# A recurrent two-tower network of 128 steps on one core: the opening's tiles, loads and orders rewritten

## The reference

```python
def _leaky(x):                      # NEG = 0.2
    return jnp.where(x >= 0, x, NEG * x)

def _tower(x, w_in, b_in, blocks):  # two blocks, all widths 128
    h = _leaky(x @ w_in + b_in)
    for w1, b1, w2, b2 in blocks:
        h = _leaky(_leaky(h @ w1 + b1) @ w2 + b2 + h)
    return h

def step(prev_delta, xk):
    fk, k = xk
    d = jnp.where(k == 0, fk[:, DELTA_IDX], jax.lax.stop_gradient(prev_delta))
    fk = fk.at[:, DELTA_IDX].set(d)
    fe = _tower(fk[:, :N_FLAT], fw_in, fb_in, flat_blocks)   # 4 features, needs d
    pe = _tower(fk[:, N_FLAT:], pw_in, pb_in, path_blocks)   # 8 features, does not
    h = _leaky(jnp.concatenate([fe, pe], axis=-1) @ cw1 + cb1)
    delta = jax.nn.sigmoid(h @ cw2 + cb2)[:, 0]
    return (delta, delta)
```

## Time and profile before

| what | us |
|---|---|
| median of 3 runs | 1250.41 |
| the three runs | 1250.08, 1250.41, 1253.89 |
| the profiled execution | 1254.54 |
| its span, first to last instruction | 1252.7 |
| PE, DVE, ACT busy in it | 1247.0, 890.9, 931.0 |

### The profile page before, as it was taken

How to read it: one execution, slowest core, us unless ns; L and a number is a source line. 1 busy time by engine, 2 the same in 40 slices (tenths; PEclk the granted TensorE clock), 3 DMA queues, 4 the chain that set the end, 5 groups by cost and what they waited for, 6 DMA issues and landing times.

```text
span 1252.7 us, 19624 instructions
## 1 busy us (share of the span) xinstructions
PE 1247.0 (100%) x6028; PEld 1063.5 (85%) x6028; DVE 890.9 (71%) x1950; ACT 931.0 (74%) x2049; POOL 11.8 (1%) x28
## 2 busy tenths in 40 slices
PE   9999999999999999999999999999999999999998
PEld 6888888888888888888888888888888888888886
DVE  3777777767777777777777777777777777777775
ACT  3777777777777777777777777777777777777776
POOL 1000000000000000000000000000000000000000
PEclk9999999999999999999999999999999999999999
DMA  2000000000000000001000000000000000000000
GB/s 75 30 10 31 13 10 30 13 30 10 24 20 11 29 13 24 17 10 33 11 23 19 12 30 10 30 13 11 29 14 29 10 21 22 11 23 12 13 4 1
DMA packets 14881, 24.50 MB, mean 20 GB/s; under 512 B 1983, under 2 KB 8214, under 8 KB 14782
## 3 DMA queue, kind: packets, MB, share of 16 engines
q1 hardware_dynamic: 13982, 22.33, 5.5%
q10 hardware_dynamic: 720, 0.66, 0.2%
q0 software_dynamic: 80, 0.26, 0.1%
HBM read 16.67 MB, written 6.55 MB: 19 GB/s over the span
## 4 chain that ended last, share of the span: by engine, by line
PE 98%; DMA 0%; ACT 0%; DVE 0%; issue 0%; ACTq 0%; DVEq 0%
PE ps_path L540 36%; PE ps_flat L540 18%; PE ps_res L543 18%; PE ps_head L670 9%; PE ps_head L665 9%; PE ps_head L683 2%; PE ps_head L678 2%; PE ps_path L570 2%; PE ps_flat L627 2%; DMA cb_col<-cb 0%; PE ps_path L565 0%; DVE f_t L448 0%; ACT delta L313 0%; DVE head_lo L482 0%; PE ps_flat L622 0%
## 5 line engine op out<-in xcount | busy, mean ns | idle before, releaser
L256 ACT ACTIVATE f_mid<-ps_flat,columns_sb 128x256 f32<-128x256 f32 x512 | 242.6, 474 | 161.9 <-PE ps_flat L540 155.5
L543 PE MATMUL ps_res<-f_mid,hidden_w 128*128 128x256 f32 x1024 | 306.1, 381 | 0.2
L540 PE MATMUL ps_path<-p_mid,hidden_w 128*128 128x256 f32 x1024 | 304.5, 380 | 0.0
L256 ACT ACTIVATE f_res<-ps_res 128x256 f32<-128x256 f32 x512 | 196.1, 384 | 62.4 <-PE ps_res L543 62.4
L540 PEld LDWEIGHTS ps_path<-p_mid,hidden_w 128*128 128x128 f32 x1024 | 190.9, 190 | 31.1 <-ACT p_mid L256 0.2
L543 PEld LDWEIGHTS ps_res<-f_mid,hidden_w 128*128 128x128 f32 x1024 | 168.6, 189 | 55.4 <-ACT f_mid L256 1.8
L414 DVE SCALAR_TENSOR_TENSOR p_sum<-ps_path,columns_sb,p_in 128x512 f32<-128x512 f32 x128 | 96.1, 751 | 126.9 <-PE ps_path L540 126.9
L256 ACT ACTIVATE p_mid<-ps_path,columns_sb 128x512 f32<-128x512 f32 x256 | 176.1, 688 | 6.4 <-PE ps_path L540 6.4
L476 DVE CAST head_hi<-head 128x256 fp32r<-128x256 f32 x256 | 75.3, 294 | 128.8 <-ACT head L256 128.7
L448 DVE SCALAR_TENSOR_TENSOR f_t<-delta,columns_sb,ps_flat 128x256 f32<-128x256 f32 x256 | 123.1, 481 | 50.0 <-ACT delta L313 48.9
L256 ACT ACTIVATE head<-ps_head,cb_scaled 128x256 f32<-128x256 f32 x256 | 121.2, 474 | 45.7 <-PE ps_head L670 39.6
(11 more groups left out here) (49 smaller groups left out, 1454.9 us busy)
## 6 DMA issues: line engine op xcount, KB each, us to landing
x_in<-x_hi SPq DMA_DIRECT2D x127, 48.0 KB
x_in<-x_lo SPq DMA_DIRECT2D x127, 48.0 KB
chunk_x<-x SPq DMA_DIRECT2D x16, 192.0 KB, 2.4
x_hi<-chunk_hi SPq DMA_DIRECT2D x16, 192.0 KB, 1.9
x_lo<-chunk_lo SPq DMA_DIRECT2D x16, 192.0 KB, 2.0
out<-delta SPq DMA_DIRECT2D x128, 2.0 KB
hidden_w<-hidden ACTq DMA_DIRECT2D x1, 384.0 KB, 5.7
hidden_w<-hidden ACTq DMA_DIRECT2D x1, 256.0 KB, 3.0
```

Source lines behind the costliest of these rows:

```text
L256: return act.activation(dst, src, ACT.Prelu, bias=bias, alpha=NEG)
L540: return pe.matmul(dst, weight[w_name], src, start=True, stop=True)
L543: return pe.matmul(dst, weight[w_name], src, start=False, stop=True, skip_group_check=True)
```

## The change

It touches the opening alone. The bodies of steps 1 to 127, and the lists of loads in them, are as before.

- `in_first`, `x_first0` and `x_first1` have 128 rows in place of 13. POOL fills `in_first` with zeros, VectorE fills the `x_first` tiles with ones (all rows, each with a semaphore of its own), and SP's loads into them wait for that. `warm` is filled on POOL in place of VectorE.
- SP's order of loads: `in_first`, then `x_first0`, the bias row, chunk 0, `x_first1`, `in_raw`, and then the late half of `hidden_w`, which was on ScalarE's queue.
- `cb2` has its own semaphore; ScalarE waits for the columns ahead of its first use of a bias and for `cb2` ahead of `delta_out(0, g)`, not at its start.
- `stay_busy(1)`, a product of ones (bf16, 256 columns) that nothing reads, stands at three places in TensorE's opening.
- The opening orders of ACT, DVE and PE are rewritten.

```diff
-        in_first = sb("in_first", [1 + FEATS, 2 * HID])
-        x_first = [sb(f"x_first{k}", [1 + FEATS, BATCH]) for k in range(WHOLE_PATH)]
+        in_first = sb("in_first", [128, 2 * HID])
+        x_first = [sb(f"x_first{k}", [128, BATCH]) for k in range(WHOLE_PATH)]
...
             def first_x(k):
+                sp.wait_ge(s_first_ones[k], 1)
                 sp.dma_start(x_first[k][1:1 + FEATS, :], x[k, :, :]).then_inc(s_x_first[k], 16)
 
+            sp.wait_ge(s_first_zero, 1)
+            sp.dma_start(in_first[1:1 + FEATS, :], w["inputs"][0:FEATS, :]).then_inc(s_in_first, 16)
             first_x(0)
-            sp.dma_start(in_first[1:1 + FEATS, :], w["inputs"][0:FEATS, :]).then_inc(s_in_first, 16)
             sp.dma_start(in_first[0:1, :], w["inputs"][FEATS:FEATS + 1, :]).then_inc(s_in_first, 16)
             load_chunk(0)
-            for k in range(1, WHOLE_PATH):
-                first_x(k)
+            first_x(1)
...
+            sp.dma_start(hidden_w[:, EARLY:], w["hidden"][:, EARLY:]).then_inc(s_w_late, 16)
             store_chunk(0)
...
         def _(pool):
+            pool.memset(warm[:, :], 1.0).then_inc(s_warm, 1)
+            pool.memset(in_first[:, :], 0.0).then_inc(s_first_zero, 1)
+            pool.dma_start(delta[1][:, :], x[0, DELTA:DELTA + 1, :].to_broadcast([HID, BATCH])).then_inc(s_delta0, 16)
+            pool.memset(in_raw[:, :], 0.0).then_inc(s_in_zero, 1)
             pool.memset(one_row[:, :], 1.0).then_inc(s_one_row, 1)
-            pool.memset(in_raw[:, :], 0.0).then_inc(s_in_zero, 1)
-            pool.dma_start(delta[1][:, :], x[0, DELTA:DELTA + 1, :].to_broadcast([HID, BATCH])).then_inc(s_delta0, 16)
...
             path_in(0)
             path_1a(0)
             flat_1a(0, 0)
+            path_1b(0)
+            flat_1b(0, 0)
             flat_1a(0, 1)
-            path_1b(0)
             path_in(1)
             flat_1b(0, 1)
-            flat_1b(0, 0)
...
-            dve.memset(warm[:, :], 1.0).then_inc(s_warm, 1)
-            for tile in x_first:
-                last = dve.memset(tile[0:1, :], 1.0)
-            last.then_inc(s_ones, 1)
+            for k in range(WHOLE_PATH):
+                dve.memset(x_first[k][:, :], 1.0).then_inc(s_first_ones[k], 1)
...
             split_first_chunk()
-            split_input_weights()
             flat_delta(0, 0)
             flat_in(0, 0)
+            split_input_weights()
+            flat_1b_old(0, 0)
             flat_delta(0, 1)
-            flat_1b_old(0, 0)
             flat_in(0, 1)
             path_1b_sum(0)
             flat_1b_old(0, 1)
-            flat_2b_old(0, 1)
             flat_2b_old(0, 0)
             split_output_weights()
+            flat_2b_old(0, 1)
             path_1b_sum(1)
             path_2b_sum(0)
+            split_chunk(1)
             path_2b(0)
-            split_chunk(1)
             path_1b_sum(2)
             head_high(0, 1)
+            head_low(0, 1)
             head_high(0, 0)
-            head_low(0, 1)
             head_low(0, 0)
...
+            def stay_busy(n):
+
+                for _ in range(n):
+                    pe.matmul(outcome(1), warm[:, 0:HID], warm[:, 0:HALF], start=True, stop=True)
+
...
             path_in(0)
             flat_x(0, 0)
+            stay_busy(1)
             path_1a(0, 0)
             path_1a(0, 1)
+            stay_busy(1)
             flat_x(0, 1)
             flat_1a(0, 0)
+            stay_busy(1)
+            output_weight_rows()
             path_1b(0, 0)
             path_1b(0, 1)
             flat_1a(0, 1)
             flat_1b(0, 0)
-            output_weight_rows()
             path_in(1)
+            path_2a(0, 0)
             flat_1b(0, 1)
-            path_2a(0, 0)
             path_1a(1, 0)
             path_1a(1, 1)
-            flat_2a(0, 0)
             path_2a(0, 1)
             flat_2a(0, 1)
+            flat_2a(0, 0)
             path_1b(1, 0)
             path_1b(1, 1)
             path_2b(0, 0)
             path_2b(0, 1)
+            flat_2b(0, 1)
+            path_in(2)
+            flat_x(1, 0)
             flat_2b(0, 0)
-            path_in(2)
-            flat_2b(0, 1)
             path_2a(1, 0)
             path_1a(2, 0)
             path_1a(2, 1)
             combine_path(0, 1)
+            path_2a(1, 1)
             combine_path(0, 0)
-            path_2a(1, 1)
             path_1b(2, 0)
             path_1b(2, 1)
             combine_flat(0, 1)
             combine_flat(0, 0)
-            flat_x(1, 0)
+            path_2b(1, 0)
+            path_in(3)
             flat_x(1, 1)
-            path_in(3)
-            path_2b(1, 0)
+            output_high(0, 1)
             path_2b(1, 1)
-            output_high(0, 1)
+            output_low(0, 1)
             output_high(0, 0)
             path_1a(3, 0)
             output_low(0, 0)
-            output_low(0, 1)
             path_1a(3, 1)
             path_2a(2, 0)
             path_2a(2, 1)
             combine_path(1, 1)
             path_1b(3, 0)
             flat_1a(1, 1)
             path_2b(2, 0)
```

More of the change, by code:

```diff
@@ L21 @@
 WARM_UP = 6
+EARLY = 4 * HID
 HIDDEN = ["pr1_w1", "fr1_w1", "pr1_w2", "fr1_w2", "pr2_w1", "fr2_w1", "pr2_w2", "fr2_w2", "cw1_flat", "cw1_path"]
@@ L117, in half @@
             return t[:, h * HALF:(h + 1) * HALF]
-        s_warm, s_ones, s_x_ones, s_in_loaded, s_in_hi, s_in_low, s_in_split, s_in_first, s_in_zero = (
-            sem(n) for n in ("s_warm", "s_ones", "s_x_ones", "s_in_loaded", "s_in_hi", "s_in_low", "s_in_split",
-                             "s_in_first", "s_in_zero"))
+        s_warm, s_x_ones, s_in_loaded, s_in_hi, s_in_low, s_in_split, s_in_first, s_in_zero, s_first_zero, s_cb2 = (
+            sem(n) for n in ("s_warm", "s_x_ones", "s_in_loaded", "s_in_hi", "s_in_low", "s_in_split",
+                             "s_in_first", "s_in_zero", "s_first_zero", "s_cb2"))
+        s_first_ones = [sem(f"s_first_ones{k}") for k in range(WHOLE_PATH)]
         s_x_first = [sem(f"s_x_first{k}") for k in range(WHOLE_PATH)]
@@ L242, in _ @@
         def _(act):
-            early = 4 * HID
-            act.dma_start(hidden_w[:, 0:early], w["hidden"][:, 0:early]).then_inc(s_w_early, 16)
+            act.dma_start(hidden_w[:, 0:EARLY], w["hidden"][:, 0:EARLY]).then_inc(s_w_early, 16)
             act.dma_start(columns_sb[:, :], w["columns"]).then_inc(s_columns, 16)
             act.dma_start(cb2_col[:, :], w["cb2"].rearrange("(p a) -> p a", a=1).to_broadcast([HID, 1]))\
-               .then_inc(s_columns, 16)
-            act.dma_start(hidden_w[:, early:], w["hidden"][:, early:]).then_inc(s_w_late, 16)
+               .then_inc(s_cb2, 16)
             cw2_at = COLUMNS.index("cw2")
@@ L252, in _ @@
             act.preload_act_table(ACT.Sigmoid)
-            act.wait_ge(s_columns, 32)
             def leaky(dst, src, bias=0.0):
@@ L264, in path_1a @@
                 if exists(k):
+                    if k == 0:
+                        act.wait_ge(s_columns, 16)
                     act.wait_ge(s_p1a_mm, k + 1)
@@ L308, in delta_out @@
                 if exists(k):
+                    if k == 0:
+                        act.wait_ge(s_cb2, 16)
                     act.wait_ge(s_out_mm[g], k + 1)
@@ L347, in _ @@
             path_in(2)
+            path_1a(2)
             flat_2b(0, 0)
             flat_2b(0, 1)
-            path_1a(2)
             path_2a(1)
@@ L356, in _ @@
             delta_out(0, 1)
+            delta_out(0, 0)
             path_1a(3)
-            delta_out(0, 0)
             path_2a(2)
@@ L384, in split_output_weights @@
             def split_output_weights():
-                dve.wait_ge(s_columns, 32)
+                dve.wait_ge(s_columns, 16)
                 dve.scalar_tensor_tensor(cw2_size[:, :], column["cw2"], -1.0, column["cw2"],
@@ L561, in path_in @@
                         if k == 0:
-                            pe.wait_ge(s_ones, 1)
                             pe.wait_ge(s_in_first, 32)
```

## The result

The changed kernel took 1256.37 us (median of 8, 1255.86 to 1257.73), the kernel before 1252.45 (median of 8 taken beside it, 1250.08 to 1254.05). The ratio is 1.0034 with a 95% interval of 1.0022 to 1.0047. The kernel before keeps its two groups of executions: in the 31 that ran beside the first four experiments, 24 took 1250.1 to 1251.2 and 7 took 1254.1 to 1254.7. Of the eight beside the changed kernel four were of the upper group, hence their median of 1252.45; against the 1250.72 of the 31 the change costs 5.65 us. The changed one has a single group above both. One later execution of the kernel before was slow (2182.2 us) and is left out of every ratio.

What follows compares the result with a forecast made beforehand. TensorE's products were taken as the bound, so only body(1)'s start counted. Span 1252.7 - 0.6 + 2.3 = 1254.4; with 1.84 around it 1256.2, without the profile's 0.65 excess 1255.6 us; range 1252.5 to 1257.6.

Steps and rivals of the forecast that it cites:

- the cast: Sign on POOL: the cast of the second chunk of features stays at 25.5 us (25.48 in the profile before).
- the order at `p_res`: Sign in VectorE's opening: `p_res` by L411 comes behind `chunk_lo` and not before it.
- The new wait at the split: VectorE's split_chunk(1), now ahead of path_2b(0), waits for the cast; TensorE pauses 5.9 us at combine_path(0, 1), until 27.35.
- The start of `path_in(0)`: TensorE's opening: begins at 4.75 us, in place of 4.13, since the bias row's load is issued 0.8 later.
- `in_low` at 9.25, so `x_in` at 11.8: VectorE and SP: input weights' split ready at about 9.25 us; x_in loads begin at 11.8, give or take 0.5, as before.
- The arrival at 21.5: TensorE reaches combine_path(0, 1) at 16.5 + r/2, 21.5 us for a rate rise at r = 10; before, 27.81.
- The fall and its price: TensorE's rate falls in the 5.9 us pause; slow products behind it cost 2.3 us, bounded by 0 and 3.1.
- The rise comes from the dense order: TensorE's opening: nearly unbroken work from 4.75 us raises the rate between 8.3 and 11, taken as 10; 128 rows cost nothing.
- The short executions of before sit on the chunk: Kernel before: short runs rise early but are held by chunk 1 at path_in(3); 3.7 us can be had, 3.8 seen.
- Rival 1: At combine_path(0, 1): the pause without the fall, or a late rise and short pause; 1253.3 us (1252.6 to 1254.1), chance 0.31.
- Behind body(1): Everything after the first product of flat_1a(1, 0), 36.10 us in the profile before, follows at a fixed distance.
- The chances: Verdict odds for the whole kernel: slower (above 1254.16 us) 0.60, within 0.37, faster (below 1246.66) 0.03.

Runs made afterwards that it cites:

- the first four experiments: The runs e1, e2, e4 and e5, edits of the changed kernel; the kernel before, run beside them, had a median of 1250.72 us.
- e1: Changed kernel with split_chunk(1) put back behind path_2b(0), its place in the kernel before: 1251.62 us.
- e2: Changed kernel with split_chunk(1) moved behind flat_in(1, 1), the last of VectorE's opening: 1249.95 us, ratio to the kernel before 0.9986.
- e5: Changed kernel with SP issuing load_chunk(1) ahead of the ten x_in loads, VectorE's order left alone: 1249.51 us, ratio to the kernel before 0.9982.
- b3: e8 with WARM_UP 8 for 6, in_first zeroed ahead of warm, cb2 and cw2-row loads behind ScalarE's table load: 1248.06 us.
- e9: Changed kernel with the kernel before's opening orders on TensorE, VectorE and ScalarE, without ones in them; tiles, fills, waits, loads kept: 1250.35 us.
- e4: Changed kernel with 50 products of ones, stay_busy(50), ahead of combine_path(0, 1) to fill TensorE's pause: 1254.87 us.
- e7: e2 with the tiles in_first, x_first0 and x_first1 of 13 rows again, all else of the change kept: 1255.25 us.
- e6: Kernel before with split_chunk(1) as the last of VectorE's opening: 1250.28 us, ratio to the kernel before 0.9993.
- e3: Kernel before with split_chunk(1) ahead of path_2b(0) on VectorE, that part of the change alone: 1254.53 us, ratio 1.0024.
- b1: e8 with WARM_UP 10 in place of 6, ten products of ones ahead of the opening: 1248.39 us, ratio to the kernel before 0.9973.
- e8: e2 without the three stay_busy(1) products of ones: 1249.08 us, ratio to the kernel before 0.9981.

## Why the prediction was right, step by step

The forecast was a loss of 5.2 us by one mechanism, a new wait and a fall of the rate behind it; 1255.6 was said, 1256.37 measured, within the range. The loss itself is 5.96 us against the 1250.41 of the forecast, 5.65 against the 31 and 3.92 against the eight beside it. Of the signs named, the cast (26.26), the order at `p_res`, a pause of 5 to 6.5 us (6.25) and 0.85 us products for 3 to 6 us behind it (4.8) held; SP's first `x_in` near 11.8 did not.

- *The new wait at the split.* Right, and shown by e1, e2 and e5 from both ends. The first head product waited for `p_res` until 28.11, predicted 27.35. The term that was short is the cast: 26.26 in place of 25.48.
- *The start of `path_in(0)`.* Mis-sized: 4.75 said, 5.78 measured. I gave the bias row's load the 2.56 us of before; it took 3.36 from its issue at 2.38. What lengthens it isn't settled: b3 issued it at 1.91 and still had it near 5.5, and in e1 and e2 it took 3.0 and 3.1.
- *`in_low` at 9.25, so `x_in` at 11.8.* Wrong by 1.0 us, outside the 0.5 I allowed: 12.81. The chain of the delay was in my own sum (the new order hangs the input weights on `flat_x(0, 0)`), and I let chunk 0's earlier landing cancel it. It did land earlier (6.73 against 7.58), but was not what the order waited for. e9 prices the step at 2.1 us of SP's queue.
- *The arrival at 21.5.* Measured 21.86, and that is luck: one more microsecond at the start and a rise at about 8.9 in place of 10 are each worth half a microsecond in that sum and cancel. The 0.4 that are left are not accounted for (the terms ahead of the wait, as printed, add up to 26.6, not 26.8).
- *The fall and its price.* Right: 2.3 said, 2.35 between the profiles of e4 and the changed kernel, though only 1.5 between their medians. No row of before showed a fall. The Trainium skill's "TensorE: Matmul & The Clock Gate" ("HAM oscillation") warns of this; the trace agrees, with the clock at 0.50 from 26.0 on after a pause that began at 21.86.
- *The rise comes from the dense order.* Wrong. I wrote that 128 rows in place of 13 change nothing, which holds for the time of a product. By e7 the rows are worth 5.3 us with the order and the ones unchanged, and by e9 the early rise comes without either. I had the hint in the rows: the stretch up to 15.2 that had no rise was followed by one-row and 13-row products, and I counted gaps but not rows.
- *The short executions of before sit on the chunk.* Not borne out (e6). The agreement of 3.7 and 3.8 us was made of two limits that happen to meet: the rise near 13.8 gives as much. Nor are all short executions of the kind that I took them for. Beside e1, 12 of the 24 have a mean granted clock of 0.997, as the traced executions with a fall of some 7 us have (e3, the changed kernel), and 11 have 1.000, like all seven long ones. e6's profile is of the second kind, with the rise near 13.8; e3's, at 0.997, shows a kind in which the rate rose before 5.3, was lost by 8 and came back near 14.8.
- *Rival 1, at 0.31,* was the same wait without the fall. e4 is its experiment, 1254.87; said were 1253.3. Of the 1.6 us between, its profile shows 0.4 for the later end of the wait, 0.2 in the list up to body(1) and 0.6 behind it; the other 0.4 is that its profile stood 0.3 above the median, where I took off 0.65.
- *Behind body(1).* I let all that follows stand at a fixed distance. It is 1216.6 us before and 1217.05 after, 0.45 more; e2, e4, e5 and e9 have 1217.2 to 1217.4, and e3 and e6, made from the kernel before, 1216.8. In the profiles 0.3 of it is lost before 200 us. No wait of its own is seen for it, and its cause stays open.
- *The chances.* The part on slower than can be told adds up to 0.62, not 0.60.

The arithmetic, against the span: 0.8 for the cast, 0.3 for the list and the rate behind it, 0.45 behind body(1) above the +1.7 predicted make the +3.2 measured. The span was missed by 1.5 us and the median only by 0.8, since the profile was the longest of the eight, 1.4 above their median, where I had taken off 0.65: that is luck too.

## What to carry to other kernels

When an opening is made faster, look for the first instruction on an in-order engine whose input comes by a DMA that the faster opening doesn't bring forward, and see who stands behind it: here a split that nobody needs until step 8 held `path_2b(0)`, the head and, through TensorE's idling, its clock. The rate of TensorE is part of that price. In this kernel it was won with products of full height (e7: 5.3 us) and with ones that last until the first data is there (b1), not with a few fillers later (e8). Where a kernel has two groups of execution times, look where the rate rises in a profile of each: here the groups went with different places of the rise, and the upper group went away with the new tiles, fills and loads in one case (e9) and with four more products of ones in the other (b1).

## What the runs showed that I had not expected

- In e7's profile 13-row products with 128-row ones between them, and hardly a pause, ran at the low rate from 5.96 to about 26; with 128-row ones in their place the changed kernel's profile had the rise at 8.9, behind a start at 5.78.
- The rate can rise just behind the products of ones and be lost again at once: in e3's profile, in which 13-row products and a pause of 0.86 us follow the ones, the clock was 1.00 from 4 to 6, 0.99 from 6 to 8 and 0.50 from 8 to 12, and the products of 5.29 took 0.59 for the pair while those of 11.12 took 1.91 for four.
- A pause of 2.7 us was enough for a fall in e1's profile, and the fall came after the pause; one of 3.0 us in e3's profile had none.
- The granted clock column of the kernel before says 1.00 in its opening although its products run at half rate there; once the clock has risen and fallen, the column shows the fall as 0.50. A 1.00 in a first stretch isn't proof of the high rate; the duration of a product is.
